# Head strips of queries and keys built by four 32-row products at a time, and q, k, v projections as three single-pass products

## The chip, the cores and the metric

## The reference

For each of 8 batch entries of 512 tokens x 256 features:

```
c   = x[b] @ cond_weight[id_b].T + cond_bias[id_b]        # weights chosen by entry
q, k, v = c @ W_Q, c @ W_K, c @ W_V                       # 16 heads of 16
att = softmax(q k^T / 4 + causal mask) v ;  x1 = x[b] + att @ W_o
h   = LoRA-FFN(x1): relu(x1 wi^T + low rank) wo^T + low rank, rank-16 parts chosen by entry
out = x1 + mixture of 8 experts of h, top 2 by a softmax gate (three layers, gelu)
```

## The kernel before, in words

Stage A is one pass per batch entry, called a round. `Round(b)` computes attention of entry b and, beside it, the FFN and the gate of entry p = b-1; there are nine rounds (round 0 has no FFN, round 8 no attention). Stage B sorts the tokens by expert, stage C runs the experts on tiles of 128 rows. The change touches stage A alone.

A round has an **opening** and then 35 attention **steps**. The opening is a hand-written list (`opening()`): `q0, k0, x1t0, x1t1, q1, k1, v0, qs0, ks0, low_i, qs1, ks1, v1, qs2, ks2, qs3, ks3`, and then four times `hid(j), qs(4+j), ks(4+j)`. Every engine walks this list in order. Item by item:

- `q`, `k` (m = 0, 1): transposed projections, 128 features x 512 tokens, two fp32 products each of `wq_raw` or `wk_sb` with `cond`, the conditioned input of this entry. ScalarE writes the high part into `parts`, VectorE then the low part, which frees the bank.
- `x1t`: output projection of the previous entry (fp32, `wo_sb` x `ot_sb`); VectorE adds the residual, ScalarE takes the high part `x_high`, VectorE the low part `x_low`.
- `v` (0, 1): two tiles of 128 tokens, fp32, four products of 256 columns; ScalarE copies them to `v_sb`.
- `qs`, `ks` (0 to 7): a strip holds two heads, 64 rows each, and repeats high and low parts so that a score product of 64 rows adds all cross terms. A strip is made by two F32R products of 512 columns with a 0/1 selection matrix `sel_sb` of 128 rows, in which only 32 rows are not zero, against `parts` (128 rows). ScalarE copies the q strips, VectorE the k strips.
- `low_i` (four F32R products of 512 columns) and `hid` (seven of them): low-rank input and hidden blocks of the FFN. ScalarE copies `low_i` first, VectorE then writes its low half; `hid` 0 waits for that. Each `hid` is taken by ScalarE (relu, high part) and then by VectorE (low part).

Between these, at places 0 and 10 of the list, ScalarE does one `cast`: it rounds a 128x512 piece of expert weights (`w_rest` to `w_high`, L961) that GpSimd has loaded. GpSimd then subtracts, writes both parts to memory and only after that loads the next piece; the cast waits for that load (`s_wpiece`). At the start of rounds 1 to 7 ScalarE also does six LoRA casts (`lora_high`) ahead of everything in the opening, and VectorE four subtractions.

A **step** has for two heads: two bf16 mask products, two score products of 64 rows (one on rows 0 to 63, the next on rows 64 to 127), transposes of earlier probabilities (L802), a piece of filler work (the rest of the FFN, and `next`: `cond` of the next entry), and every other step probabilities times v. VectorE takes row maxima (`nmax`, L1238), ScalarE the exponential (`probs`, L1060). The first score waits until all strips and v have left PSUM.

Banks are dealt out by `psum_plan`: the opening takes banks 0, 1, 2, 3, 7 in turn; a product waits (`vacant`) until its bank's last content is gone. Scores use banks 0 to 2, fillers 3 and 7, transposes 4 and 5, probabilities times v bank 6 (`PV_BANK`).

Of the kernel before, what the change touches and what calls it, by code (L numbers as in the profile page):

```python
# [18 lines left out]
F32 = mybir.dt.float32  # L19
# [8 lines left out]
P = 128  # L28
# [61 lines left out]
PT_SLOTS = 6  # L90

# [24 lines left out]
def opening(attends, feeds):  # L116

    strips = [[(w, g) for w in ("qs", "ks")] for g in range(HC)]
    order = [] if feeds else [("cond", o) for o in range(KD)]  # L120
    order += [("q", 0), ("k", 0), ("x1t", 0), ("x1t", 1), ("q", 1), ("k", 1), ("v", 0)]
    order += strips[0] + [("low_i", 0)] + strips[1] + [("v", 1)] + strips[2] + strips[3]
    for j in range(HID_EARLY):
        order += [("hid", j)] + strips[4 + j]
# [4 lines left out]
def psum_plan(attends, feeds, leads):  # L129
# [3 lines left out]
    rings = {"linear": [0, 1, 2, 3, 7], "score": [0, 1, 2], "filler": [3, 7], "t": [4, 5],  # L133
# [68 lines left out]
def build_kernel(nc, xT, x_cond_w, x_cond_b, itok, wq, wk, wv, wo, wi_t, wo_t, lora_at, lora_wb, lora_ao, lora_bo,  # L202
# [8 lines left out]
    with outer:  # L211
# [17 lines left out]
        with attn:  # L229
# [7 lines left out]
            cond = sb("cond", [P, KD, S], F32, attn)  # L237
# [3 lines left out]
        behind_attn = sb("behind_attn", [P, PT_SLOTS - 4, S], F32)  # L241
# [5 lines left out]
        wq_raw = sb("wq_raw", [P, KD, D], F32, part_a)  # L247
        wk_sb = sb("wk_sb", [P, KD, D], F32, part_a)
        wv_sb = sb("wv_sb", [P, KD, D], F32, part_a)
        wo_sb = sb("wo_sb", [P, KD, D], F32, part_a)  # L250

        sel_sb = sb("sel_sb", [P, 4, 4, P], F32R, part_a)
# [36 lines left out]
        with ExitStack() as shared:  # L289
            sel_f = sb("sel_f", [P, 4, 4, P], F32, shared)  # L290
# [21 lines left out]
        weight_space = sb("weight_space", [P, 2 * W_ALL - (PT_SLOTS - 4) * S], F32)  # L312
# [92 lines left out]
        s_prep = sem("s_prep")  # L405
        s_idb = sem("s_idb")
# [94 lines left out]
        def _(sp):  # L501
# [93 lines left out]
            sp.dma_start(wk_sb[:, :, :], wk).then_inc(s_const, 16)  # L595
            sp.dma_start(wv_sb[:, :, :], wv).then_inc(s_const, 16)
            sp.dma_start(id_f[:, :], ident).then_inc(s_const, 16)
            sp.dma_start(mask_f[:, :], maskd).then_inc(s_const, 16)
            sp.dma_start(sel_f[:, :, :, :], sel).then_inc(s_sel_f, 16)
# [46 lines left out]
        def _(pe):  # L646
# [6 lines left out]
            def product(rd, n, piece=None):  # L653
# [19 lines left out]
                elif what in ("q", "k"):  # L673
# [4 lines left out]
                    w = wq_raw if what == "q" else wk_sb  # L678
                    for k in range(KD):
                        ins = mm(dst()[:, :], w[:, k, m * P:(m + 1) * P], cond[:, k, :],  # L680
                                 start=(k == 0), stop=(k == KD - 1))
                elif what == "v":
                    vacant(pe, n, rd)
                    for u in range(2):
                        t = 2 * m + u
                        for k in range(KD):
                            ins = mm(dst()[:, u * D:(u + 1) * D], cond[:, k, t * P:(t + 1) * P], wv_sb[:, k, :],
                                     start=(k == 0), stop=(k == KD - 1))
                elif what in ("qs", "ks"):
# [76 lines left out]
            def turn(rd):  # L766
                b, p = rd.b, rd.p
                for n in rd.opening:
                    if p is None and n == ("q", 0):
                        pe.wait_ge(s_const, 16 * N_CONST)  # L770
                        pe.wait_ge(s_idb, 1)
                        pe.wait_ge(s_prep, 1)
# [183 lines left out]
        def _(act):  # L956
# [6 lines left out]
            def take(rd, n, piece=None):  # L963
# [3 lines left out]
                if what == "cond" or what == "next" and piece == KD - 1:  # L967
# [3 lines left out]
                    ins = nc.scalar.activation(cond[:, m, :], at(n, rd)[:, :], ACT.Identity, bias=bc_sb[:, m:m + 1])  # L971
# [59 lines left out]
            def turn(rd):  # L1031
# [3 lines left out]
                for n in rd.opening:  # L1035
                    if p is None and n == ("q", 0):
# [601 lines left out]
```

## Time and profile before

| | |
|---|---|
| median of 3 runs (lowest, highest) | 1537.2 us (1536.48, 1538.39) |
| the profiled execution: its time, its span | 1538.85 us, 1537.3 us |
| TensorE busy | 1416.1 us, 92% |
| VectorE, ScalarE, GpSimd busy | 864.5, 764.6, 419.1 us |
| mean granted TensorE clock | 0.945 |

A granted clock of 1.00 is 2.4 GHz and 0.50 is 1.2 GHz. In a timeline each row gives start and duration in us, engine, line of the kernel, instruction, out<-in and count; square brackets hold the idle time before it and what ended it. The duration of a matmul includes its way through the array, so products that follow each other densely overlap: the distance between starts is what one costs.

### The profile page before, as it was taken

What the parts mean: (1) busy time and instruction counts of PE and PEld (TensorE: products, weight loads), DVE (VectorE), ACT (ScalarE), POOL (GpSimd) and SP (SyncE); (2) the same over time, 40 slices, a digit from 0 to 9 for tenths busy, and PEclk for the clock granted to TensorE, in tenths of its full rate; (3) what the DMA queues carried; (4) which work ended last, traced back from release to release, by engine and by line L of the source; (5) the groups of instructions that cost most, each with busy time, mean ns of one, the idle gap of its engine ahead of it and who ended that gap; (6) DMA issues with size and microseconds to landing.
All of it is one profiled execution on the core that took longest, in us unless ns stands there. A gap on an engine that the chain in (4) does not pass through costs nothing.

```text
span 1537.3 us, 31909 instructions
## 1 busy us (share of the span) xinstructions
PE 1416.1 (92%) x10169; PEld 1085.2 (71%) x10170; DVE 864.5 (56%) x1927; ACT 764.6 (50%) x2000; POOL 419.1 (27%) x553
## 2 busy tenths in 40 slices
PE   6989999999999999999999998339999999999997
PEld 3556776776776776776776776237878888888886
DVE  2665665665665665665664663464555555555554
ACT  3675665665665665665664663003333333333332
POOL 2222211211211211221221220033344544444442
PEclk9599999999999999999999999659999999999998
DMA  6121222222222222222222220381624222442221
GB/s 237 62 83 56 77 84 90 77 84 90 77 84 90 77 84 90 76 84 90 77 84 69 77 78 28 158 332 35 230 58 142 43 40 50 138 145 40 40 38 13
DMA packets 50642, 138.62 MB, mean 90 GB/s; under 512 B 10515, under 2 KB 29587, under 8 KB 48755
## 3 DMA queue, kind: packets, MB, share of 16 engines
q0 software_dynamic: 28992, 68.35, 16.2%
q1 hardware_dynamic: 21554, 68.97, 12.1%
q8 instruction: 64, 1.05, 0.3%
q14 instruction: 32, 0.25, 0.1%
HBM read 86.82 MB, written 51.38 MB: 90 GB/s over the span
## 4 chain that ended last, share of the span: by engine, by line
PE 83%; DVE 5%; DMA 4%; ACT 3%; issue 3%; POOL 1%; POOLq 0%; SPq 0%; DVEq 0%; ACTq 0%
PE bank L651 68%; PE bank L802 10%; PE bank L895 4%; ACT probs L1060 2%; DMA xg<-hrows,gid 1%; PE bank L887 1%; DMA wsplit<-w_rest 1%; DMA out<-y_sb,sid 1%; DVE nmax L1238 1%; DMA w_rest<-in_w_all 1%; PE bank L810 0%; DVE probs_t L1252 0%; POOL hit_v L1496 0%; ACT w_high L961 0%; POOL w_rest L1476 0%
## 5 line engine op out<-in xcount | busy, mean ns | idle before, releaser
L1060 ACT ACTIVATE probs<-bank,nmax 128x512 f32<-128x512 f32 (+3 forms) x512 | 266.0, 525 | 171.0 <-DVE nmax L1238 169.5
L1238 DVE TENSOR_REDUCE nmax<-bank 128x1 f32<-128x512 f32 (+3 forms) x512 | 227.3, 486 | 209.3 <-PE bank L651 209.0
L1094 ACT ACTIVATE g<-z 128x512 f32<-128x512 f32 x142 | 89.8, 632 | 279.5 <-DVE z L1426 279.5
L1476 POOL TENSOR_TENSOR w_rest<-w_rest,w_high 128x512 f32<-128x512 f32 x64 | 81.4, 1271 | 467.7 <-ACT w_high L961 467.7
L802 PE MATMUL bank<-id_f,probs 128*128 128x128 f32 x1280 | 202.9, 290 | 0.2
L651 PE MATMUL bank<-wst,g1t_high 128*128 x568 | 185.3, 407 | 0.9 <-DVE g1t_low L1414 0.9
L802 PEld LDWEIGHTS bank<-id_f,probs 128*128 128x128 f32 x1280 | 138.4, 143 | 44.0 <-issue 27.0
L1518 POOL DMA_INDIRECT out<-y_sb,sid x71 | 114.3, 1609 | 150.1 <-DVE y_sb L1447 69.1
L1252 DVE COPY probs_t<-bank 128x128 f32<-128x128 f32 (+3 forms) x320 | 140.3, 454 | 9.1 <-PE bank L802 9.1
L1426 DVE TENSOR_TENSOR z<-bank,b_sb 128x512 f32<-128x512 f32 x142 | 98.2, 691 | 72.5 <-PE bank L651 61.1
L651 PEld LDWEIGHTS bank<-wst,g1t_high 128*128 128x128 f32 x568 | 102.2, 190 | 20.8 <-issue 1.1
L651 PE MATMUL bank<-wst,g1t_low 128*128 x284 | 113.0, 398 | 0.0
L651 PE MATMUL bank<-wst,g2t_high 128*128 x568 | 108.4, 290 | 1.5 <-DVE g2t_low L1414 1.5
L651 PE MATMUL bank<-k_sb,q_sb 64*128 64x512 f32 (+3 forms) x512 | 108.8, 422 | 0.0
L651 PE MATMUL bank<-mask_b,id_b 128*128 128x128 bf16 x512 | 83.0, 229 | 21.2 <-ACT probs L1060 10.1
L651 PE MATMUL bank<-probs_t,v_sb 128*32 128x128 f32 x2560 | 102.3, 289 | 0.0
L1060 ACT ACTIVATION_READ_ACCUMULATOR probs<-bank,nmax 128x1 f32 x512 | 101.4, 198 | 0.0
L651 PE MATMUL bank<-wst,xgt_high 128*128 x284 | 96.0, 420 | 1.3 <-DVE xgt_low L1414 1.1
L1508 POOL DMA_INDIRECT xg<-hrows,gid x71 | 76.0, 1071 | 63.9 <-POOL gid L1505 57.7
L1068 ACT COPY probs_t<-bank 128x384 f32<-128x384 f32 (+3 forms) x192 | 88.3, 460 | 6.8 <-PE bank L802 6.8
L651 PEld LDWEIGHTS bank<-mask_b,id_b 128*128 128x128 bf16 x512 | 35.3, 98 | 79.7 <-issue 50.4
L1473 POOL DMA_DIRECT2D w_rest<-in_w_all x64 | 34.8, 544 | 206.4 <-DMA wsplit<-w_rest 206.4
(193 smaller groups left out, 2921.2 us busy)
## 6 DMA issues: line engine op xcount, KB each, us to landing
wst<-wsplit SPq DMA_DIRECT2D x8, 4096.0 KB, 12.5
w_rest<-in_w_all POOLq DMA_DIRECT2D x64, 256.0 KB, 3.0
wsplit<-w_high POOLq DMA_DIRECT2D x64, 256.0 KB, 2.3
wsplit<-w_rest POOLq DMA_DIRECT2D x64, 256.0 KB, 2.6
hrows<-h_sb SPq DMA_DIRECT2D x8, 528.0 KB, 3.0
x_in<-in_xT SPq DMA_DIRECT2D x8, 512.0 KB, 3.5
wb_raw<-in_lora_wb SPq DMA_DIRECT2D x8, 512.0 KB, 3.5
x_res<-in_xT SPq DMA_DIRECT2D x8, 512.0 KB, 3.3
```

The lines of the kernel that those rows point to most:

```text
L651: return nc.tensor.matmul(*a, **k)
L802: ins = nc.tensor.transpose(at(n, rd)[:, kb * P:(kb + 1) * P], probs[:, t % 4, kb * P:(kb + 1) * P], id_f[:, :])
L895: ins = nc.tensor.transpose(bank[bt][:, k * P:(k + 1) * P], g[:, k * P:(k + 1) * P], id_f[:, :])
L1060: taken(nc.scalar.activation(probs[:, s % 4, 0:(i + 1) * P], at(n, rd)[:, 0:(i + 1) * P], ACT.Exp, bias=nmax[:, s % 8:s % 8 + 1], accum_ou ...
L1068: taken(nc.scalar.copy(probs_t[:, t % PT_SLOTS, 0:w], at(n, rd)[:, 0:w]), n, rd)
L1094: nc.scalar.activation(g[:, :], z[:, :], ACT.Gelu).then_inc(s_g, 1)
L1238: V.tensor_reduce(nmax[:, s % 8:s % 8 + 1], at(n, rd)[:, 0:(s // HEADS + 1) * P], AX.X, ALU.max, negate=True).then_inc(s_max, 1)
L1252: taken(V.tensor_copy(probs_t[:, t % PT_SLOTS, 0:w], at(n, rd)[:, 0:w]), n, rd)
L1426: V.tensor_tensor(z[:, :], bank[bl][:, :], bias[:, bass.ds(e, 1), :].rearrange("p o n -> p (o n)"), ALU.add).then_inc(s_z, 1)
L1476: nc.gpsimd.tensor_tensor(w_rest[:, :], w_rest[:, :], w_high[:, :].bitcast(F32), ALU.subtract).then_inc(s_wlow, 1)
L1508: nc.gpsimd.indirect_dma_start(xg[:, buffer, :], None, hrows, bass.IndirectOffsetOnAxis(ap=gid[:, 0:1], axis=0), bounds_check=B * S - 1, o ...
L1518: nc.gpsimd.indirect_dma_start(out_rows, bass.IndirectOffsetOnAxis(ap=sid[:, 0:1], axis=0), y_sb[:, buffer, :], None, bounds_check=B * S - ...
```

## The change

The query and key strips are no longer made one by one. `opening()` puts four of one kind together (`quads`): a strip's selection matrix and its part of `parts` are cut to the 32 rows that count, strip number `pair` of a quad reads rows 32 pair to 32 pair + 31, and the four write four different banks. A quad is eight F32R products of 32 rows x 512 columns, first the four of the high part, then the four of the low part. The order becomes `q0, k0, x1t0, x1t1, q1, k1, v0, qs0-3, low_i, ks0-3, hid0, v1, qs4-7, hid1, ks4-7, hid2, hid3`. The opening's ring has eight banks now. ScalarE copies the strips with even numbers, VectorE those with odd ones. `cast` keeps its places 0 and 10 in the list of single items.

`cond` is kept as `cond_high` (ScalarE) and `cond_low` (VectorE, a new instruction of 128x512 for each of its two blocks per round, which now frees the bank). `wq`, `wk`, `wv` are split into high and low parts once, in round 0 (three ScalarE and three VectorE instructions in place of one VectorE scaling). Each projection product of fp32 becomes three F32R products. The selection matrices shrink from 128x2048 to 128x512. The rest of the diff, not shown, is declarations, the loads' new names and the sizes of shared SBUF spaces.

```diff
@@ -116,12 +117,11 @@
-    strips = [[(w, g) for w in ("qs", "ks")] for g in range(HC)]
+    quads = [[(w, 4 * c + pair) for pair in range(4)] for c in range(KD) for w in ("qs", "ks")]
     order = [] if feeds else [("cond", o) for o in range(KD)]
     order += [("q", 0), ("k", 0), ("x1t", 0), ("x1t", 1), ("q", 1), ("k", 1), ("v", 0)]
-    order += strips[0] + [("low_i", 0)] + strips[1] + [("v", 1)] + strips[2] + strips[3]
-    for j in range(HID_EARLY):
-        order += [("hid", j)] + strips[4 + j]
+    order += quads[0] + [("low_i", 0)] + quads[1] + [("hid", 0), ("v", 1)] + quads[2] + [("hid", 1)] + quads[3]
+    order += [("hid", j) for j in range(2, HID_EARLY)]
     ours = ("cond", "q", "k", "v", "qs", "ks")
...
@@ -130,7 +130,7 @@
-    rings = {"linear": [0, 1, 2, 3, 7], "score": [0, 1, 2], "filler": [3, 7], "t": [4, 5],
+    rings = {"linear": [0, 1, 2, 3, 7, 4, 5, PV_BANK], "score": [0, 1, 2], "filler": [3, 7], "t": [4, 5],
              "pv": [PV_BANK]}
...
@@ -675,24 +687,40 @@
                     vacant(pe, n, rd, [("cond", o) for o in range(KD)] if n == ("q", 0) and p is None else ())
-                    w = wq_raw if what == "q" else wk_sb
+                    if p is None and m == 0:
+                        pe.wait_ge(s_prep, 1 if what == "q" else 2)
+                    w_high, w_low = (wq_high, wq_low) if what == "q" else (wk_high, wk_low)
                     for k in range(KD):
-                        ins = mm(dst()[:, :], w[:, k, m * P:(m + 1) * P], cond[:, k, :],
-                                 start=(k == 0), stop=(k == KD - 1))
+                        for w, x in ((w_high, cond_high), (w_high, cond_low), (w_low, cond_high)):
+                            ins = mm(dst()[:, :], w[:, k, m * P:(m + 1) * P], x[:, k, :],
+                                     start=(k == 0 and w is w_high and x is cond_high), stop=(k == KD - 1 and w is w_low))
                 elif what == "v":
                     vacant(pe, n, rd)
+                    if p is None and m == 0:
+                        pe.wait_ge(s_prep, 3)
                     for u in range(2):
                         for k in range(KD):
-                            ins = mm(dst()[:, u * D:(u + 1) * D], cond[:, k, t * P:(t + 1) * P], wv_sb[:, k, :],
-                                     start=(k == 0), stop=(k == KD - 1))
+                            for x, w in ((cond_high, wv_high), (cond_high, wv_low), (cond_low, wv_high)):
+                                ins = mm(dst()[:, u * D:(u + 1) * D], x[:, k, t * P:(t + 1) * P], w[:, k, :],
+                                         start=(k == 0 and x is cond_high and w is wv_high),
+                                         stop=(k == KD - 1 and x is cond_low))
                 elif what in ("qs", "ks"):
                     c, pair = divmod(m, 4)
+                    if pair:
+                        return
                     slot = 0 if what == "qs" else 2
-                    vacant(pe, n, rd, [(what[0], c)])
+                    quad = [(what, m + pair) for pair in range(4)]
+                    for pair in range(4):
+                        vacant(pe, quad[pair], rd, [(what[0], c)] if pair == 0 else ())
                     for u in range(2):
-                        ins = mm(dst()[:, :], sel_sb[:, slot + u, pair, :], parts[:, c, slot + u, :],
-                                 start=(u == 0), stop=(u == 1))
+                        for pair in range(4):
+                            rows = slice(PART * pair, PART * (pair + 1))
+                            ins = mm(at(quad[pair], rd)[:, :], sel_sb[rows, slot + u, :], parts[rows, c, slot + u, :],
+                                     start=(u == 0), stop=(u == 1))
+                            if u == 1:
+                                done(ins, quad[pair], rd)
+                    return
                 elif what == "low_i":
...
@@ -968,7 +995,9 @@
                     filled(act, n, rd)
-                    ins = nc.scalar.activation(cond[:, m, :], at(n, rd)[:, :], ACT.Identity, bias=bc_sb[:, m:m + 1])
+                    nc.scalar.activation(cond_high[:, m, :], at(n, rd)[:, :], ACT.Identity, bias=bc_sb[:, m:m + 1]
+                                         ).then_inc(s_cond_high, 1)
+                    return
                 elif what in ("q", "k"):
...
@@ -979,9 +1008,9 @@
                         ins = nc.scalar.copy(v_to[:, :, half, :, half, :], v_ps[:, :, half, :, :])
-                elif what == "qs":
+                elif what in ("qs", "ks") and m % 2 == 0:
                     filled(act, n, rd)
-                    ins = nc.scalar.copy(q_sb[:, m, :], at(n, rd)[:, :])
+                    ins = nc.scalar.copy((q_sb if what == "qs" else k_sb)[:, m, :], at(n, rd)[:, :])
                 elif what == "x1t":
...
@@ -1038,9 +1067,13 @@
                         act.wait_ge(s_vzero, 1)
+                        nc.scalar.activation(wq_high[:, :, :], wq_raw[:, :, :], ACT.Identity, scale=DH ** -0.5
+                                             ).then_inc(s_prep_high, 1)
+                        nc.scalar.copy(wk_high[:, :, :], wk_raw[:, :, :]).then_inc(s_prep_high, 1)
+                        nc.scalar.copy(wv_high[:, :, :], wv_raw[:, :, :]).then_inc(s_prep_high, 1)
                     if p is None and n == ("qs", 0):
                         act.wait_ge(s_sel_f, 16)
-                        nc.scalar.copy(sel_sb[:, :, :, :], sel_f[:, :, :, :]).then_inc(s_sel, 1)
+                        nc.scalar.copy(sel_sb[:, :, :], sel_f[:, :, :]).then_inc(s_sel, 1)
                     take(rd, n)
...
@@ -1125,9 +1158,6 @@
             V = nc.vector
-            dve.wait_ge(s_const, 16 * N_CONST)
-            V.tensor_scalar(wq_raw[:, :, :].rearrange("p k n -> p (k n)"), wq_raw[:, :, :].rearrange("p k n -> p (k n)"),
-                            DH ** -0.5, None, ALU.mult).then_inc(s_prep, 1)
             dve.sem_inc(s_hout, 1)
...
@@ -1153,15 +1183,19 @@
                 b, p = rd.b, rd.p
-                if what in ("q", "k"):
+                if what == "cond" or what == "next" and piece == KD - 1:
+                    dve.wait_ge(s_cond_high, (b if what == "cond" else b + 1) * KD + (m + 1))
+                    ins = V.scalar_tensor_tensor(cond_low[:, m, :], at(n, rd)[:, :], bc_sb[:, m:m + 1],
+                                                 cond_high[:, m, :].bitcast(F32), ALU.add, ALU.subtract)
+                elif what in ("q", "k"):
                     slot = 0 if what == "q" else 2
                                                  at(n, rd)[:, :], ALU.mult, ALU.add)
-                elif what == "ks":
+                elif what in ("qs", "ks") and m % 2 == 1:
                     filled(dve, n, rd)
-                    ins = V.tensor_copy(k_sb[:, m, :], at(n, rd)[:, :])
+                    ins = V.tensor_copy((q_sb if what == "qs" else k_sb)[:, m, :], at(n, rd)[:, :])
                 elif what == "low_i":
...
@@ -1218,6 +1252,12 @@
                 for before, n in zip([None] + rd.opening, rd.opening + [None]):
+                    if p is None and n == ("q", 0):
+                        for w, (low, raw, high) in enumerate(((wq_low, wq_raw, wq_high), (wk_low, wk_raw, wk_high),
+                                                              (wv_low, wv_raw, wv_high))):
+                            dve.wait_ge(s_prep_high, w + 1)
+                            V.scalar_tensor_tensor(low[:, :, :], raw[:, :, :], DH ** -0.5 if w == 0 else 1.0,
+                                                   high[:, :, :].bitcast(F32), ALU.mult, ALU.subtract).then_inc(s_prep, 1)
                     if n == ("low_i", 0):
...
@@ -1613,8 +1653,7 @@
-        "sel": _np.stack([_np.stack([_np.kron(_np.eye(4)[:, pair:pair + 1], _np.kron(_np.eye(2),
-                                              _np.kron(rows, _np.eye(DH)))) for pair in range(4)], axis=1)
+        "sel": _np.stack([_np.tile(_np.kron(_np.eye(2), _np.kron(rows, _np.eye(DH))), (4, 1))
                           for rows in ([[1, 0, 1, 0]], [[0, 1, 0, 1]], [[1, 1, 0, 0]], [[0, 0, 1, 1]])],
```

## Rows read from the trace of the kernel before

**Rows 1.** The page: busy time of TensorE, and the clock in 40 slices.

```profile
PE 1416.1 (92%) x10169; PEld 1085.2 (71%) x10170; DVE 864.5 (56%) x1927; ACT 764.6 (50%) x2000; POOL 419.1 (27%) x553
...
PEclk9599999999999999999999999659999999999998
```

**Rows 2.** Windows: stretch; busy us of PE, PEld, DVE, ACT, POOL; clock, DMA share, GB/s.

```profile
39.20:76.80 37.60, 36.28 (x223) 21.37 (x223) 25.08 (x72) 24.79 (x92) 8.68 (x12) 0.50 0.18 63
226.90:233.80 6.90, 6.15 (x27) 2.63 (x20) 3.69 (x12) 4.76 (x9) 0.00 (x0) 0.51 0.30 94
238.00:261.00 23.00, 21.83 (x89) 16.39 (x87) 11.86 (x18) 10.55 (x21) 3.45 (x5) 1.00 0.24 85
```

**Rows 3.** Timeline of TensorE in the opening of round 2 and its first steps.

```profile
228.48 3.75 PE L651 MATMUL bank<-cond,wq_raw 128*128 128x512 f32 x4 [0.75 <-issue]
...
234.61 3.60 PE L651 MATMUL bank<-ot_sb,wo_sb 128*128 128x512 f32 x8
238.05 1.88 PE L651 MATMUL bank<-cond,wq_raw 128*128 128x512 f32 x4
...
245.06 1.09 PE L651 MATMUL bank<-parts,sel_sb 128*128 128x512 f32 x4
245.98 1.89 PE L651 MATMUL bank<-wv_sb,cond 128*128 128x256 f32 x8
...
258.75 1.08 PE L651 MATMUL bank<-parts,sel_sb 128*128 128x512 f32 x4
261.12 0.27 PE L651 MATMUL bank<-mask_b,id_b 128*128 128x128 bf16 x2 [1.29 <-DVE k_sb L1164]
...
262.37 0.38 PE L651 MATMUL bank<-mask_b,id_b 128*128 128x128 bf16 x2
```

**Rows 4.** Timeline of TensorE in steps: score pairs and what stands around them.

```profile
198.84 0.50 PE L651 MATMUL bank<-k_sb,q_sb 64*128 64x512 f32 x2
199.28 0.88 PE L802 MATMUL bank<-id_f,probs 128*128 128x128 f32 x6
199.91 0.36 PE L651 MATMUL bank<-wf_high,hid_high 128*128 128x256 f32 x1
200.11 0.28 PE L651 MATMUL bank<-wf_low,hid_high 128*128 128x256 f32 x1
...
200.71 0.46 PE L651 MATMUL bank<-mask_b,id_b 128*128 128x128 bf16 x2
...
264.14 0.28 PE L651 MATMUL bank<-mask_b,id_b 128*128 128x128 bf16 x2
264.35 0.33 PE L651 MATMUL bank<-k_sb,q_sb 64*128 64x128 f32 x2
264.61 0.33 PE L802 MATMUL bank<-id_f,probs 128*128 128x128 f32 x1
```

**Rows 5.** Timeline of the weight loads of one of these score pairs.

```profile
198.84 0.19 PEld L651 LDWEIGHTS bank<-k_sb,q_sb 64*128 64x128 f32 x2
```

**Rows 6.** Timeline of ScalarE, VectorE and GpSimd in round 2.

```profile
233.78 0.62 ACT L961 CAST w_high<-w_rest 128x512 fp32r<-128x512 f32 x1
...
216.96 1.29 DVE L1238 TENSOR_REDUCE nmax<-bank 128x1 f32<-128x512 f32 x2 [1.65 <-PE bank L651]
...
245.88 0.68 DVE L1168 SCALAR_TENSOR_TENSOR low_i<-bank,low_i 32x512 fp32r<-32x512 f32 x1 [0.86 <-ACT low_i L991]
...
240.39 0.54 POOL L1473 DMA_DIRECT2D w_rest<-in_w_all  x1 [2.77 <-DMA wsplit<-w_rest]
```

**Rows 7.** The page: loads of expert weight pieces, KB each, us to landing.

```profile
w_rest<-in_w_all POOLq DMA_DIRECT2D x64, 256.0 KB, 3.0
```

**Rows 8.** Timeline of round 0, TensorE and ScalarE.

```profile
16.00 1.96 PE L651 MATMUL bank<-cond,wq_raw 128*128 128x512 f32 x4 [1.93 <-ACT mask_b L1039]
...
37.80 0.27 PE L651 MATMUL bank<-mask_b,id_b 128*128 128x128 bf16 x2 [0.98 <-DVE k_sb L1164]
...
25.40 1.91 ACT L1043 CAST sel_sb<-sel_f 128x2048 fp32r<-128x2048 f32 x1
```

More of the change, by code:

```diff
@@ L90 @@
 PT_SLOTS = 6
+BEHIND = PT_SLOTS - 4 + KD
 def place_of(h):
@@ L236, in build_kernel @@
             x_in = sb("x_in", [P, KD, S], F32, attn)
-            cond = sb("cond", [P, KD, S], F32, attn)
+            cond_high = sb("cond_high", [P, KD, S], F32R, attn)
+            cond_low = sb("cond_low", [P, KD, S], F32R, attn)
         with ExitStack() as weights:
@@ L240, in build_kernel @@
         attn_space = sb("attn_space", [P, 2, 2, W_ALL], F32)
-        behind_attn = sb("behind_attn", [P, PT_SLOTS - 4, S], F32)
+        behind_attn = sb("behind_attn", [P, BEHIND, S], F32)
         x_res = sb("x_res", [P, KD, S], F32, part_a)
@@ L246, in build_kernel @@
         bc_sb = sb("bc_sb", [P, KD], F32, part_a)
-        wq_raw = sb("wq_raw", [P, KD, D], F32, part_a)
-        wk_sb = sb("wk_sb", [P, KD, D], F32, part_a)
-        wv_sb = sb("wv_sb", [P, KD, D], F32, part_a)
+        with ExitStack() as shared:
+            wq_raw = sb("wq_raw", [P, KD, D], F32, shared)
+        wq_low = sb("wq_low", [P, KD, D], F32R, part_a)
+        wq_high = sb("wq_high", [P, KD, D], F32R, part_a)
+        with ExitStack() as shared:
+            wk_raw = sb("wk_raw", [P, KD, D], F32, shared)
+        wk_low = sb("wk_low", [P, KD, D], F32R, part_a)
+        wk_high = sb("wk_high", [P, KD, D], F32R, part_a)
+        with ExitStack() as shared:
+            wv_raw = sb("wv_raw", [P, KD, D], F32, shared)
+        wv_low = sb("wv_low", [P, KD, D], F32R, part_a)
+        wv_high = sb("wv_high", [P, KD, D], F32R, part_a)
         wo_sb = sb("wo_sb", [P, KD, D], F32, part_a)
-        sel_sb = sb("sel_sb", [P, 4, 4, P], F32R, part_a)
+        sel_sb = sb("sel_sb", [P, 4, P], F32R, part_a)
         nmax = sb("nmax", [P, 8], F32, part_a)
@@ L289, in build_kernel @@
         with ExitStack() as shared:
-            sel_f = sb("sel_f", [P, 4, 4, P], F32, shared)
+            sel_f = sb("sel_f", [P, 4, P], F32, shared)
         hid_low = sb("hid_low", [P, KF, S], F32R, part_a)
@@ L309, in build_kernel @@
         part_a.close()
-        weight_space = sb("weight_space", [P, 2 * W_ALL - (PT_SLOTS - 4) * S], F32)
+        weight_space = sb("weight_space", [P, 2 * W_ALL - BEHIND * S], F32)
         tri_f = sb("tri_f", [P, P], F32)
@@ L405, in build_kernel @@
         s_prep = sem("s_prep")
+        s_prep_high = sem("s_prep_high")
+        s_cond_high = sem("s_cond_high")
         s_idb = sem("s_idb")
@@ L594, in _ @@
             load_in(0, e0)
-            sp.dma_start(wk_sb[:, :, :], wk).then_inc(s_const, 16)
-            sp.dma_start(wv_sb[:, :, :], wv).then_inc(s_const, 16)
+            sp.dma_start(wk_raw[:, :, :], wk).then_inc(s_const, 16)
+            sp.dma_start(wv_raw[:, :, :], wv).then_inc(s_const, 16)
             sp.dma_start(id_f[:, :], ident).then_inc(s_const, 16)
             sp.dma_start(mask_f[:, :], maskd).then_inc(s_const, 16)
-            sp.dma_start(sel_f[:, :, :, :], sel).then_inc(s_sel_f, 16)
+            sp.dma_start(sel_f[:, :, :], sel).then_inc(s_sel_f, 16)
             sp.dma_start(wo_sb[:, :, :], wo).then_inc(s_mid, 16)
@@ L771, in turn @@
                         pe.wait_ge(s_idb, 1)
-                        pe.wait_ge(s_prep, 1)
                     if p is None and n == ("qs", 0):
```

## Prediction

> **What bounds the kernel now.** I read the page first: TensorE is busy 92% of the span, and its clock reads 9 in all slices but two, so this engine paces the kernel [rows 1]. Then I took windows over stage A. In the opening of round 2 the clock is full and TensorE busy for 21.8 of 23.0 us, ScalarE for 10.6 and VectorE for 11.9 [rows 2]: every microsecond taken from TensorE there counts until one of the other two is late. The windows also show two kinds of half-clock stretches. One of 37.6 us covers the attention of round 0, which has no filler work. One of 6.9 us lies over the start of round 2, behind the sparse end of round 1, and loses 3.4 us; rounds 3 to 7 each have one of the same length [rows 2]. Last I read the timeline of one opening. Between q0 at 228.48 and the second step's masks at 262.37 TensorE stands still once, 1.29 us before the first score, for the last k strip: VectorE copies it behind the low part of `hid` 3 [rows 3]. That point, 33.9 us after q0, is where I compare.
>
> **Prices.** Four full-width single-pass products take 0.92 us, 0.23 each (245.06 to 245.98). Eight records of fp32 products take 3.44 us, 0.43 each (234.61 to 238.05) [rows 3]. Single-pass products of 256 columns take 0.12: five between 200.11 and 200.71 [rows 4].
>
> **Projections.** A q or k item is four records, 1.72 us; it becomes six products, 1.38. Four items save 1.36 us per opening. A v item has as many columns, 1.72 us, and becomes twelve products of 256, 1.44; two items save 0.56. The single-pass price is that of the same form of product with the same weight load, so I give this little doubt.
>
> **Strips.** Before, 16 strips are 32 products of 0.23: 7.36 us. For 32-row products there is no row; the nearest are the score pairs, two 64-row products on the two halves of the array. Such a pair needs 0.44 us at 512 columns (198.84 to 199.28) and 0.26 at 128 (264.35 to 264.61) [rows 4]. The 384 columns between cost 0.18, or 0.24 for 512: the price of one product, not of two, so the pair runs at the same time. Its two weight loads take 0.19 us together, the length of one [rows 5], so loads on different rows go together as well. What the pair costs beyond its columns is 0.20 us, and its neighbours pay too: the two masks in front take 0.21 us where two products of 128 columns need 0.11 (264.14 to 264.35), and the first product after the transposes 0.20 where the next ones need 0.12 [rows 4]. A visit to the narrow form costs 0.20 + 0.10 + 0.08 = 0.38 us. A quad is one visit with two rounds of 512 columns: 0.46 + 0.38, about 0.83 us, if four overlap as two do and the second four weights load under the first four products. Four quads: 3.3 us, 4.1 less per opening. Bounds: 0.60 (half the visit hidden) and, if the weights of the four load one after the other at 0.11 (what a transpose costs with its 128-column load: six between 199.28 and 199.91), 8 x 0.11 + 0.38 = 1.2; without any overlap 8 x 0.23 + 0.1 = 1.9. I take 0.83, the value of the pair.
>
> The Trainium skill, "TensorE: Matmul & The Clock Gate", in its part on packing small matmuls, gives 3.07 times for four 32-row products of 512 columns. By it a quad would take 1.84 / 3.07 = 0.60 us and the total below would be 1497; the case has no four-fold row yet.
>
> **What is late next.** I laid the new list out by hand for round 2, with the rows' durations, VectorE to TensorE 0.24 us (as ahead of 261.12), and ScalarE held by its LoRA casts until its cast at 233.78 as before [rows 6]. (The same table for the old list puts the second step's masks at 262.39; the row says 262.37.) TensorE: q0 228.5, k0 231.2 (both mostly at half clock), x1t 233.7, q1 237.2, k1 238.6, v0 239.9, first q quad 241.4, `low_i` 242.2, first k quad 243.1, done at 243.9. Then comes `hid` 0, and it waits for the low half of `low_i`. Before, three strip pairs and v1 lay between; now only one quad does. The chain: ScalarE has the second cast at place 10, ahead of its `low_i` copy. The piece's load is issued 240.39 and lands after 3.0 us, 243.4 [rows 6, 7], 14.9 us after q0. Cast 0.5 us, `low_i` copy 0.6, VectorE's low half 0.69, semaphore 0.24: `hid` 0 starts at 245.5 instead of 243.9, a new stall of 1.6 us. Then `hid` 0, v1, quad, `hid` 1, quad and `hid` 2, 3 run without gaps to 255.0; all banks they need were copied out over 0.5 us before. The strips' copies lie under `hid` 2 and 3, so the old wait of 1.29 us goes. The second step comes sooner than its bank: VectorE must write the low part of `hid` 3 (to 256.4) before the first row maximum, the exponential ends near 257.1, and the second step's masks wait about 0.9 us, to 257.2. So 262.4 becomes 257.2: 5.1 us in round 2. By terms: 1.36 + 0.56 + 4.1 + 0.4 (1.3 wait to 0.9) less 1.6, and 0.3 for the part saved at half clock.
>
> The same table for the other rounds, each with its own half-clock stretch: 5.1, 5.1, 4.6, 4.9, 4.5 us in rounds 3 to 7. Round 1 has no half-clock stretch, reaches `hid` 0 about 2.4 us earlier after q0 and so waits 4.0 us for the same load: 2.6 us saved. Sum of rounds 1 to 7: 31.8 us.
>
> **Round 0.** Here the list has no FFN work. The preparation grows: three ScalarE casts of 0.5 us behind the mask cast and VectorE's first low part put q0 at 17.3 instead of 16.00. The four items and v0 then end at 24.2. The selection cast, 1.91 us before the first strip, falls to 0.6 [rows 8]. From 25.7 the quads are paced by the copies, four banks each, two copies on VectorE at 0.61, and end in a first score at 32.9 instead of 37.80: 4.9 us. The pauses may let the clock fall before the first score and not after 1.4 us of it, 0.4 less. I take 4.5.
>
> **Hidden at no price.** VectorE's two `cond_low` per round (0.69 each) fall into steps where it idles 1.65 us between maxima [rows 6]; if that cover were gone, 0.7 us each, 10 us in all. Later drains of the `next` banks delay nothing that is due within 2 us. Splitting the weights is counted in round 0. Stages B and C keep their code. A smaller selection load only frees DMA time. More banks in the opening cost nothing: the transposes' banks and bank 6 are idle then.
>
> **Sum.** 31.8 + 4.5 = 36.3 us. The profiled execution took 1538.85 us (span 1537.3 and 1.55 around it), which gives 1502.5; the median of the runs lies 1.65 lower, so 1500.9.
>
> **Rivals.**
> 1. *All removed work shows.* If the load lands earlier, or the copies pass faster, so that `hid` 0 doesn't wait, an opening saves 6.4 + 0.3 us: 7 x 6.7 + 5 = 52, 1485. For it: TensorE had no such wait before. Against: the chain is 2.0 us long behind the load with one quad of 0.83 as cover. A half-clock stretch that disappears from the rounds' starts (3.4 us each) would mostly be eaten by the same wait.
> 2. *The four overlap in part.* Weight loads in series, 1.2 us a quad: rounds 1 to 7 save 25.2, 1507.5. No overlap, 1.9 us: 11.6, 1521. For it: a transpose costs its weight load, not its columns; against: [rows 5].
> 3. *Slower: weights exposed.* If the products go one by one and each load (0.19) stands in front, a quad takes 8 x 0.42 + 0.38 = 3.7 us, 1.9 more than before. Per opening 7.5 lost against 2.3 saved by the rest: 7 x 5.2 - 4.5 = 32 slower, 1569. It turns slower once a quad costs over about 2.5 us. Against: both rows of the score pairs.
> 4. *Slower: the clock.* The new waits (4.0 us in round 1, 1.6 later) stand in a stretch that was dense; what precedes each fall of the clock now is a sparse piece of some us. One stretch as in [rows 2] costs 3.4 us; slower than before needs over 5.2 us per opening, that is two of them in each of seven, about 1545. For it: round 0's attention stayed at half clock for 37.6 us. Against: after 1.29 us of idling at 261.12 the clock stayed at 1.00. One extra stretch in round 1 alone is inside my range.
> 5. *PSUM copies pace the opening.* If every quad had to wait for copies, it would cost two VectorE copies, 1.22 us, instead of 0.83: 1.6 more per opening, 11 in all, 1512. Against: VectorE has 21 passes of 0.61 and 2.3 us of LoRA in the new opening, 15 of 28.7 us, so I expect this in round 0 alone. The Trainium skill, "TensorEngine Tiling (Array Packing)", section "PSUM Bottleneck", warns that the copies can become the bound once TensorE is four times as fast.
>
> **How the numbers follow.** Forecast 0.59, with its own range 1493 to 1509 (quad 0.60 to 1.2, clock edges moved by one stretch or two); all work shows 0.14; partial overlap 0.13; copies 0.03; no change 0.02; clock 0.05; exposed weights 0.04. The range 1484 to 1518 takes in the first two, the copies and most of the partial overlap, and leaves out about 0.15. 0.2% (3 us) is what a measurement can tell. Faster 0.89, same 0.02, slower 0.09.
>
> **What would show it.** A quad: start of its first product to the next item, 0.83 us. A gap before `hid` 0 of 1.6 us (4 in round 1), ended by VectorE's `low_i`. No gap before the first score, 0.9 us before the second step's masks. q0 of round 0 at 17.3, its first score at 32.9. Rounds 2 to 7 some 111 us apart instead of 116. The prediction is wrong if the quad's products don't overlap, if half-clock stretches multiply or vanish, or if attention steps get longer by VectorE's new work.

## The result, and the profile after

The changed kernel takes 1527.4 us at the median (1519.1 to 1533.3, 11 runs), the kernel before 1538.0 in the same series (11 runs). The ratio is 0.9926, with an interval of 0.9903 to 0.995: some 11 us are gained where 36 were forecast. The interval leaves out 1.000, so there is a gain, but the time lies outside the range of the prediction, on its slow side. Below, times are compared by such ratios.

The profiled execution took 1528.85 us with a span of 1527.2, 10.1 us less than before. The page of it, first TensorE's busy time and then the clock in 40 slices, answers to [rows 1]:

```profile
PE 1377.0 (90%) x10297; PEld 1069.8 (70%) x10298; DVE 874.2 (57%) x1945; ACT 764.4 (50%) x2003; POOL 419.2 (27%) x553
...
PEclk8799999999999999999999999559999999999999
```

TensorE is busy 39 us less, but the span shrinks by a quarter of that: TensorE now stands where it did not. The timeline of TensorE in the opening of round 2 shows where, and answers to [rows 3]:

```profile
225.32 0.77 PE L663 MATMUL bank<-cond_high,wq_high 128*128 128x512 f32 x1 [0.76 <-issue]
...
237.04 0.28 PE L663 MATMUL bank<-wv_high,cond_low 128*128 128x256 f32 x1
237.25 0.74 PE L663 MATMUL bank<-parts,sel_sb 32*128 32x512 f32 x8
237.93 0.50 PE L663 MATMUL bank<-x_high,at_cat 128*128 128x512 f32 x1
238.26 0.40 PE L663 MATMUL bank<-x_low,at_cat 128*128 128x512 f32 x1
...
239.06 0.74 PE L663 MATMUL bank<-parts,sel_sb 32*128 32x512 f32 x8
244.79 0.77 PE L663 MATMUL bank<-x_high,wi_high 128*128 128x512 f32 x1 [4.99 <-issue]
...
256.25 0.28 PE L663 MATMUL bank<-mask_b,id_b 128*128 128x128 bf16 x2
...
257.53 0.23 PE L663 MATMUL bank<-mask_b,id_b 128*128 128x128 bf16 x1
258.51 0.23 PE L663 MATMUL bank<-mask_b,id_b 128*128 128x128 bf16 x1 [0.76 <-ACT probs L1093]
258.67 0.33 PE L663 MATMUL bank<-k_sb,q_sb 64*128 64x128 f32 x2
```

Ahead of `hid` 0 (244.79) TensorE stands for 4.99 us; the forecast had 1.6. Of the second step's two mask products the first starts at 257.53, and the second waits for its bank to 258.51, 33.19 us after q0, where 28.7 was forecast. The score behind them is the place where like can be compared with like. It starts 33.35 us after q0, and in the kernel before, in the row below, 34.20:

```profile
262.68 0.33 PE L651 MATMUL bank<-k_sb,q_sb 64*128 64x128 f32 x2
```

So the opening of round 2 gains 0.85 us and not 5.1. Over rounds 1 to 7 the wait ahead of `hid` 0 is 4.60, 4.99, 4.59, 3.30, 1.20, 4.46 and 3.86 us. "Issue" says only that the profile names no releaser; ScalarE and VectorE show it. Their timelines, in round 2:

```profile
242.86 0.62 ACT L988 CAST w_high<-w_rest 128x512 fp32r<-128x512 f32 x1 [3.77 <-DMA w_rest<-in_w_all]
243.38 0.59 ACT L1020 ACTIVATE low_i<-bank 128x512 fp32r<-128x512 f32 x1
...
244.00 0.68 DVE L1202 SCALAR_TENSOR_TENSOR low_i<-bank,low_i 32x512 fp32r<-32x512 f32 x1 [4.67 <-ACT low_i L1020]
```

The chain is the one of the prediction: load, cast, `low_i` copy, low half, `hid` 0. But the load is late. GpSimd's timeline answers to [rows 6], and SyncE's follows it:

```profile
233.93 0.54 POOL L1521 DMA_DIRECT2D wsplit<-w_rest  x1
239.78 0.54 POOL L1513 DMA_DIRECT2D w_rest<-in_w_all  x1 [5.32 <-DMA wsplit<-w_rest]
```

```profile
233.95 0.34 SPq L541 DMA_DIRECT2D x_res<-in_xT  x1
```

GpSimd issues the next piece's load only when its two writes have landed. It waits 5.32 us for them where it waited 2.77 [rows 6], and so the load leaves 14.46 us after q0 instead of 11.91. The second write goes out at 233.93. The 512 KB load of the residual, `x_res`, is issued at 233.95, behind the last reader of `x_res`. In the kernel before it was issued 10.56 us after q0, behind the writes; now it is at 8.63 us, on top of them. The table of DMA issues for 225 to 245 gives the landing times: the write took 5.1 us, and 2.6 at the same place before.

```profile
x_res<-in_xT SPq DMA_DIRECT2D x1, 512.0 KB, 4.4
...
wsplit<-w_rest POOLq DMA_DIRECT2D x1, 256.0 KB, 5.1
w_rest<-in_w_all POOLq DMA_DIRECT2D x1, 256.0 KB, 3.0
```

The second loss is the clock. Windows of round 2, columns as in [rows 2]: while TensorE stands the granted clock falls to 0.50 and stays there for 6.8 us, 3.9 of them with work.

```profile
235.40:242.00 6.60, 4.39 (x35) 2.90 (x33) 3.04 (x5) 2.31 (x5) 0.54 (x1) 0.99 0.50 153
241.90:248.70 6.80, 3.91 (x11) 3.29 (x12) 1.97 (x3) 2.62 (x5) 2.35 (x3) 0.50 0.23 86
248.70:256.30 7.60, 7.60 (x48) 5.39 (x47) 4.56 (x7) 4.04 (x9) 0.54 (x1) 1.00 0.11 35
```

A stretch of half clock stands at this place in rounds 1, 2, 3, 4, 6 and 7, of 3.4 us in rounds 1 and 4 and of 6.8 us in the others. The kernel before has none there. Round 5 is the exception: its q0 fell 0.9 us into the half-clock stretch at the round's start, so 6.0 us of it came behind q0 (2.9 in round 2), TensorE reached x1 later, and `x_res` was issued 10.04 us after q0, behind the writes. GpSimd's timeline of it, then TensorE's:

```profile
582.36 0.54 POOL L1513 DMA_DIRECT2D w_rest<-in_w_all  x1 [2.79 <-DMA wsplit<-w_rest]
```

```profile
587.50 0.47 PE L663 MATMUL bank<-x_high,wi_high 128*128 128x512 f32 x1 [1.20 <-issue]
```

There the load leaves at 11.92, `hid` 0 starts at 17.06 (forecast: 17.0), no stretch follows, the waiting mask product comes at 28.98 after q0, and the score behind it 4.5 us sooner after q0 than before. The forecast had 4.6. One round in seven went as predicted.

### The profile page after: what moved, and what is told of

Same layout as the page of the kernel before. It is cut to its first block, busy times and chain, and to the rows that moved or that the text cites. A ratio compares the mean times of both kernels' runs of the same rounds, so it can differ in the third digit from the quotient of the medians.

```text
span 1527.2 us, 32247 instructions
## 1 busy us (share of the span) xinstructions
PE 1377.0 (90%) x10297; PEld 1069.8 (70%) x10298; DVE 874.2 (57%) x1945; ACT 764.4 (50%) x2003; POOL 419.2 (27%) x553
## 4 chain that ended last, share of the span: by engine, by line
PE 80%; DMA 5%; DVE 5%; issue 5%; ACT 4%; POOL 1%; POOLq 0%; SPq 0%; DVEq 0%; ACTq 0%
PE bank L663 65%; PE bank L829 9%; PE bank L922 4%; ACT probs L1093 2%; DMA wsplit<-w_rest 1%; DMA w_rest<-in_w_all 1%; DMA out<-y_sb,sid 1%; PE bank L914 1%; DMA xg<-hrows,gid 1%; DVE nmax L1278 1%; PE bank L837 0%; POOL hit_v L1536 0%; DVE probs_t L1292 0%; POOL w_rest L1516 0%; ACT w_high L988 0%
```

## The experiments

No experiment leaves out part of the computation. The theory, A: TensorE waits for the cast behind a late load, the load is late by the `x_res` collision, and the clock falls because TensorE stands. The rivals: the cast's place is not the point, the collision is not, or the 32-row products themselves bring the clock down.

**1. The cast late.** The opening's second `cast` goes from place 10 of the list to place 17, right behind v1. ScalarE has then copied `low_i` and `hid` 0 before it waits for the load.

```diff
-W_OPENING = (0, 10)
+W_OPENING = (0, 17)
```

> The changed kernel with one edit: ScalarE's second cast of an expert weight piece moves from place 10 of the opening's list (behind the first quad) to place 17 (behind v1). Base: ratio 0.9926 to the kernel before, 1527 us; TensorE waits 27.1 us in all ahead of hid 0 in rounds 1 to 7 (1.2 to 5.0 each) and six half-clock stretches that the kernel before does not have begin at those waits (17.1 us lost). Theory A (ScalarE stands at the cast for the piece's load, low_i's copy is queued behind it, and the clock falls because TensorE stands still): the wait ahead of hid 0 falls to about 1.1 us per round, the second half-clock stretch of rounds 1 to 7 is gone, 19 + 17 = 36 us less, about 1491, ratio 0.970. Theory B (the low_i chain is too long for one quad of cover whatever the cast does): the waits stay, ratio 0.99. Theory C (the clock falls because the 32-row quads count for little, not because of the waits): waits go, the half-clock stretches stay, about 1508, ratio 0.981.

Measured: 0.9702 (0.9676 to 0.9727). The wait ahead of `hid` 0 is 0.78 us in every round, and no half-clock stretch follows it; TensorE's timeline and a window, round 2:

```profile
241.03 0.47 PE L663 MATMUL bank<-x_high,wi_high 128*128 128x512 f32 x1 [0.78 <-issue]
```

```profile
241.00:248.00 7.00, 6.97 (x45) 5.16 (x46) 3.79 (x6) 4.21 (x10) 1.69 (x2) 1.00 0.00 0
```

Against the changed kernel that is 2.2%, some 34 us, three times what the change had brought. In the profiled executions, which differ by 32.5 us of span, the waits ahead of `hid` 0 are 21.5 us shorter in sum, and the half clock behind them, worth 12.3 us, is gone. Two smaller parts are not the wait's: the half-clock stretches at the starts of rounds 2 to 7 last 27.3 us in sum instead of 37.5, worth up to 5 us, and the half clock of round 0's attention lasts longer, so that round 1 starts 5.8 us later.

**2. The residual's load late.** It waits for the copies of x1 in the attention steps too, which puts it some 48 us after q0, far behind GpSimd's writes; the cast stays at place 10.

```diff
+                    wait_for(rd, free, x1s, v_x1)
                     if rd.b is not None:
                         wait_for(rd, free, x1ts, v_x1t)
                         load_res(rd.b)
-                    wait_for(rd, free, x1s, v_x1)
```

> The changed kernel with one edit: SyncE issues the 512 KB load of x_res for the next round behind its wait for the x1 copies (in the attention steps) and not right after x1t has been taken, where it now falls 0.02 us behind GpSimd's second write of a weight piece. The cast keeps place 10. Theory A (that load delays the writes, GpSimd waits 4 to 5 us for them where it waited 2.8 before, and the piece's load and the cast come later): GpSimd's wait returns to 2.8 us, the load lands 14.9 us after q0, the wait ahead of hid 0 is 4.0 us in round 1 and about 1.6 in rounds 2 to 7, 13.5 us less in all, and the half-clock stretches of rounds 2 to 7 go with it (15 us): about 1499, ratio 0.975. Rival (the writes are slow for another reason): no change, 0.9926.

Measured: 0.9839 (0.9813 to 0.9865), 0.9% or some 13 us better than the changed kernel, but less than expected. That the collision held the writes up is shown: GpSimd's wait falls to 2.76 to 2.78 us in six of seven rounds, and in these the cast starts 14.8 to 15.0 us after q0, as forecast (13.8 in round 1). In round 2 the wait is 3.74 us with no `x_res` near; what held that write up stays open. Round 3, where q0 is at 337.99: GpSimd, ScalarE, TensorE, and windows.

```profile
349.89 0.54 POOL L1513 DMA_DIRECT2D w_rest<-in_w_all  x1 [2.76 <-DMA wsplit<-w_rest]
```

```profile
352.95 0.62 ACT L988 CAST w_high<-w_rest 128x512 fp32r<-128x512 f32 x1 [0.99 <-DMA w_rest<-in_w_all]
```

```profile
354.88 0.47 PE L663 MATMUL bank<-x_high,wi_high 128*128 128x512 f32 x1 [2.22 <-issue]
```

```profile
354.80:358.80 4.00, 3.92 (x13) 3.35 (x14) 1.64 (x3) 0.82 (x2) 1.21 (x3) 0.57 0.37 135
358.80:364.80 6.00, 6.00 (x40) 4.21 (x39) 3.52 (x6) 3.49 (x8) 0.54 (x1) 1.00 0.13 44
```

What the expectation missed: the wait of 2.1 to 3.1 us that is left still brings half clock behind it, in every one of the seven rounds, each stretch 3.4 us long. With the load landing as forecast (rounds 3 to 7) TensorE waits 2.07 to 2.44 us and not 1.6, and half clock follows. What a wait of 1.6 us would do in an opening no run shows.

**3. The wait filled.** 18 extra products of 512 columns stand ahead of `hid` 0, into its bank; their result is overwritten. TensorE then doesn't stand, but nothing is done sooner.

```diff
+FILL = 18
...
+                    if m == 0 and b is not None:
+                        vacant(pe, n, rd)
+                        for _ in range(FILL):
+                            mm(dst()[:, :], wi_high[:, 0, 0:P], x_high[:, 0, :], start=True, stop=True)
```

> The changed kernel with 18 extra F32R products of 512 columns (4.1 us, result overwritten) on TensorE right ahead of hid 0 in rounds 1 to 7, into hid 0's own bank. Nothing else moves. Theory A (the clock falls because TensorE stands still for 4 to 5 us): the half-clock stretches behind this place are gone, 17 us, and the products cost only in round 5, where the wait is 1.2 us (3 us more): about 1513, ratio 0.984. Theory C (the clock falls for the quads' sake): the stretches stay, about 1530, ratio 0.995.

Measured: 0.9876 (0.9853 to 0.99). The window over the place where the clock was at 0.50, and the products (the 19th is the first of `hid` 0):

```profile
242.00:248.00 6.00, 6.00 (x38) 4.86 (x37) 2.67 (x4) 3.15 (x7) 2.40 (x3) 1.00 0.24 87
```

```profile
240.10 4.61 PE L664 MATMUL bank<-x_high,wi_high 128*128 128x512 f32 x19
```

The clock stays at 1.00 at this place in all rounds, with the same quads before it. So the standing brings it down, not the narrow products. The whole program gains less than the openings show, because in this execution the half clock of round 0's attention lasts 41.0 us instead of 20.5, which is 10 us lost.

**4. The cast late, and v1 ahead of `hid` 0**, to cover the last 0.78 us.

```diff
-... + quads[1] + [("hid", 0), ("v", 1)] + quads[2] ...
+... + quads[1] + [("v", 1), ("hid", 0)] + quads[2] ...
```

> The edit of e1 (cast at place 17) and v1 put ahead of hid 0 in the opening's list. Theory A: v1's twelve products (1.44 us) cover what is left of the wait for low_i's low half, about 7 us less than e1 over seven rounds: 1484, ratio 0.965. Theory B: no gain over e1.

Measured: 0.9691 (0.9669 to 0.9714). The wait is gone; against experiment 1 the intervals overlap, so a gain is not shown.

**5. The strips alone.** The quads with the cast late, and the projections left in fp32 as before; the edit, not shown, is the strips' part of the change and the cast's place.

> The strips' part of the change alone, with the cast at place 17: quads, their order in the list, eight banks, small selection matrices; the q, k, v projections stay fp32 as before. Theory A (quads measured at 0.68 us in the changed kernel's trace): strips 7.36 to 2.7 us per opening, 1.29 to 0.75 ahead of the attention, about 0.8 given back ahead of hid 0: 4.3 us in each of seven rounds and 4 in round 0, 34 us, about 1505, ratio 0.978. The difference to e1 (0.9702) is then what the projections give: 1.9 us in seven rounds less the later start of round 0. Rival (the projections' products carry the gain): ratio above 0.985.

Measured: 0.979 (0.9762 to 0.9818). The strips with the cast late bring 2.1%. The difference to experiment 1, 0.9%, is the share of the projections; the intervals do not overlap, but the two were measured in different series. The quad stands in the same place in both and costs the same. In this kernel's round 2:

```profile
230.61 1.89 PE L650 MATMUL bank<-wv_sb,cond 128*128 128x256 f32 x8
232.43 0.73 PE L650 MATMUL bank<-parts,sel_sb 32*128 32x512 f32 x8
233.10 0.50 PE L650 MATMUL bank<-x_high,at_cat 128*128 128x512 f32 x1
```

**6. The quad strip by strip.** Experiment 1, with high and low product of a strip behind each other instead of four high ones and then four low ones. If four products on different rows must stand side by side to overlap, this undoes it.

```diff
-                    for u in range(2):
-                        for pair in range(4):
+                    for pair in range(4):
+                        for u in range(2):
```

> e1 with the quad's eight products in another order: both products of strip 0, then both of strip 1, and so on (same instructions, same rows and banks). Theory A (products on different rows run together, two on the same rows one after the other, and TensorE takes them in order): the second product of one strip runs beside the first of the next, five lengths of 0.23 us in place of two, a quad takes about 1.35 us instead of 0.68; 0.7 x 4 x 8 = 21 us more than e1, about 1515, ratio 0.984. Rival (each row group has its own queue, order is indifferent): as e1, 0.970.

Measured: 0.9713 (0.9693 to 0.9733), the same as experiment 1, and the quad takes 0.68 us:

```profile
234.49 0.75 PE L663 MATMUL bank<-parts,sel_sb 32*128 32x512 f32 x8
235.17 0.50 PE L663 MATMUL bank<-x_high,at_cat 128*128 128x512 f32 x1
```

My expectation was wrong and the rival's right: the order inside the group doesn't matter here.

**7. The split of the weights early.** Experiment 4, with ScalarE and VectorE splitting `wq` and `wk` before the first `cond` is ready, and `wv` behind it. The edit, not shown, moves only these instructions and two small casts.

> e4 (cast at place 17, v1 ahead of hid 0) with round 0's preparation moved: ScalarE splits wq and wk and writes the bf16 identity and mask before it takes the first conditioned block, wv right after them, and VectorE's low parts of wq and wk go ahead of cond_low. TensorE waits 3.23 us for wq_low in e4 (q0 at 17.46). Theory: q0 starts about 16.4, 1 us earlier, and the half-clock stretch of 18 to 23 (1.7 us) may go: 1 to 3 us less than e4, ratio 0.967 to 0.969. Rival: the start is set by the cond products and their copies, q0 not earlier than 17.0, no change.

Measured: 0.9671 (0.9651 to 0.969). q0 of round 0 starts at 15.47 at full clock, not at 17.40 at half clock (17.46 in experiment 4). It has now only `cond` to wait for:

```profile
15.47 0.48 PE L663 MATMUL bank<-cond_high,wq_high 128*128 128x512 f32 x1 [1.76 <-DVE cond_low L1189]
```

Round 1 then starts 1.7 us sooner than in experiment 4, within what was expected, but the intervals of the two ratios overlap, so a gain over experiment 4 is not shown.

**8. A control.** The kernel before, with its cast moved to place 17 of its own list, which is `hid` 0; the cast runs behind that copy (the expectation says just ahead of it).

> The kernel before the change, with only the place of the opening's second cast moved: from place 10 of its list to place 17, the place just ahead of its own first hidden block. A control for the experiment that moved the cast in the changed kernel and took it from 0.993 to 0.970. Theory A (the cast's place matters only because the change made TensorE arrive at hidden block 0 early and wait there; before the change three pairs of strips and v1 lay between, and no wait was there): 1.000, between 0.997 and 1.003, and no wait ahead of hidden block 0 as before. Rival (a late cast helps any such opening, by freeing ScalarE for its copies or by another course of the clock): 0.990 or less, the start of the second step then earlier than 30.2 to 33.1 us after the round's start.

Measured: 0.9999 (0.9985 to 1.0013). The move is worth nothing without the quads: three strip pairs and v1 covered the chain there. What experiment 1 gained is thus the price of a wait that the change itself had opened.

**9. Experiment 7, and the residual's load late** as in experiment 2.

> The best version so far (cast late, v1 ahead of hidden block 0, weights of round 0 split earlier; 0.967), and in it the 512 KB residual load issued late as well, behind the same wait as in the earlier experiment. Theory A (the collision of this load with GpSimd's writes costs only through the cast that TensorE waited for; with the cast late nobody waits): 0.967, between 0.964 and 0.970, though GpSimd's wait for its writes falls from about 5 to about 3 us. Rival (the collision also delays later pieces, or holds GpSimd back in the steps): 0.964 or less.

Measured: 0.9629 (0.9612 to 0.9646), which lies below the range of theory A and on the rival's side of the expectation. It is the lowest ratio of this study, 3% below that of the changed kernel. GpSimd's load is issued 11.9 us after q0 again, where experiment 7 had it at 13.4:

```profile
227.90 0.54 POOL L1516 DMA_DIRECT2D w_rest<-in_w_all  x1 [2.76 <-DMA wsplit<-w_rest]
```

The profiled executions of experiments 7 and 9 differ by 0.6 us of span and start rounds 1 to 7 within 0.5 us of each other. So the traces show nothing of what the rival names, a delay of later pieces that costs time, and where the difference of 0.4% between their ratios comes from stays open; the two were measured in different series.

## Why the prediction was wrong, by its own steps

**The failed step** is that of "What is late next", with rival 4 behind it. It took the load as issued 11.9 us after q0, as in the kernel before, and so landing 14.9 after it. The duration was right (3.0 to 3.2 us). The issue was not: in rounds 1 to 7 the load leaves 12.8, 14.5, 14.1, 13.1, 11.9, 14.0 and 13.6 us after q0. I had laid out TensorE, VectorE and ScalarE for the new list, but not SyncE, whose `x_res` load moves forward with x1. The load moves by 1.93 us in round 2: 0.66 for q0 and k0, which are shorter, and some 1.2 because more of the half-clock stretch now lies ahead of q0. The 0.66 alone would have put it at 9.90, and in the kernel before round 7 has it at 9.88 with a wait of GpSimd of 2.85 us, so that much would have passed; the margin was what I should have looked for. The trace of the kernel before had it in round 1, which has no such stretch: q0 is at 115.28, `x_res` is issued 7.96 us after it, and GpSimd already waits 3.86 us there. SyncE, then GpSimd, of the kernel before:

```profile
123.24 0.34 SPq L529 DMA_DIRECT2D x_res<-in_xT  x1
```

```profile
127.11 0.54 POOL L1473 DMA_DIRECT2D w_rest<-in_w_all  x1 [3.86 <-DMA wsplit<-w_rest]
```

The prediction took round 2's load for all rounds. With the load put back to its forecast time (experiment 2) the kernel gains some 13 us, half of what was missing; the other half is the clock, below, and a wait that was longer than 1.6 us even then.

What it cost, in the profiled executions: `hid` 0 was to start 17.0 us after q0 in every round; it starts at 17.77, 19.47, 19.10, 17.99, 17.06, 19.02 and 18.65, 10.1 us late in sum. The waits themselves are longer than forecast by 13.4 us; part of that is only earlier arrival.

**The clock**, rival 4, was no term of the sum: what follows a new wait was put at nothing, and the rival had been given 0.05 with "two of them in each of seven" as its condition for a slower kernel. One in six rounds came. Behind the six waits TensorE works at half clock from `hid` 0 to the rise for 3.4, 3.9, 4.4, 2.9, 4.6 and 5.5 us, which loses half of it, 12.3 us. My argument against it was the 1.29 us of idling ahead of the first score; experiment 2 shows how little that argument covered: 2.07 us were enough, and the 4.0 us that I had forecast for round 1 lay far above that. (The rival's 1545 is a slip besides: two stretches of 3.4 us in seven rounds are 47.6 us, 1548 in all.) The text had named one such stretch, in round 1, as within its range, and not asked why only there.

**The sum.** Late `hid` 0, 10.1; half clock behind it, 12.3; more of the rounds' first half-clock stretches lying ahead of q0, 1.6; round 0, 0.5; stages B and C, 2.3. Together 26.8 us; 1502.5 forecast for the profiled execution and 1528.85 measured differ by 26.3. The last 2.3 us lie in stage C, whose code did not change: from its first product with `wst` to the end the changed kernel takes 500.8 us and the kernel before 498.4. Over the eleven profiled executions of this study, all with the same code there, that part takes 498.1 to 502.2 us, so this is probably a difference between executions.

**The terms that held.** The projections cost 0.23 and 0.12 us a product (in round 2 six of k1 in 1.40 us, from 234.35 to 235.75, and twelve of v0 in 1.41), and are worth 0.9% (experiment 5); 1.92 us by seven rounds is 13.4 us, 0.9%. The quad was priced at 0.83 with what it does to its neighbours. It takes 0.68 from its start to the next item, 0.09 in front (237.04 to 237.25 where 0.12 is a product) and 0.10 behind (237.93 to 238.26 where 0.23 is one): 0.87. The sign named in the prediction, "start of its first product to the next item, 0.83", mixed the two. The quad's 0.68 is 2.7 times as fast as eight products one by one (1.84), and its 0.87 with the neighbours 2.1 times. By the 3.07 times of the Trainium skill, "TensorE: Matmul & The Clock Gate", part on packing small matmuls, the estimate for a quad was 0.60; the trace has 0.68, and the measurement decides. Round 0, where two quads follow each other without a gap, is in line with a price made of a visit and the columns:

```profile
28.64 1.20 PE L663 MATMUL bank<-parts,sel_sb 32*128 32x512 f32 x16 [1.25 <-ACT sel_sb L1076]
```

One quad's row lasts 0.74 us and two last 1.20, so the second adds 0.46, the price of two products for eight. With the wait out of the way (experiment 1) the changes are worth 3.0%; the forecast was 2.4% with 14 us of waits in it.

**The wait before the second step's masks**, forecast 0.9, is 0.75 to 0.76 in all rounds. No round waits ahead of the first score.

**Round 0.** q0 at 17.40 (17.3 forecast), the masks of the first score at 35.14, not at 32.9 (37.80 before): in the pause of 2.79 us ahead of q0 the clock fell, at 16.6, and it rose at 23.4, in a stretch I had taken as full. The half clock of round 0's attention lasts 20.5 us, not 37.5, and another stretch of 6.8 us stands at 84.9. Round 1 starts 4.0 us sooner; I had 4.5. That this is close is in part luck: only 2.7 us were gained by the first score, and the long half-clock stretch behind it differs from execution to execution. In the control (experiment 8), whose round 0 has the work of the kernel before, it lasts 23.9 us and round 1 starts 3.4 us sooner as well.

**The other rivals.** Weights are not exposed: the eight loads of a quad take 0.30 us together. This is the timeline of weight loads, and answers to [rows 5]:

```profile
237.25 0.30 PEld L663 LDWEIGHTS bank<-parts,sel_sb 32*128 32x128 f32 x8
```

Copies pace the openings nowhere but in round 0.

## What to carry to other kernels

When one engine's work is shortened, lay out the new times of every queue, also of those that only issue transfers: a load that moves forward by 2 us can land on a write that somebody waits for. Put an instruction that waits for a transfer behind the copies that the bounding engine needs next; here one number in a list was worth three times the change. A short new wait on TensorE is to be priced with the clock that follows it, in each round and not in one.

## What the runs showed of the hardware that I had not expected

- In a dense stretch, waits of 2.07 to 3.10 us (seven in experiment 2) were each followed by half clock for 3.4 us; waits of 0.78 us (seven in experiment 1), 1.20 us (round 5 of the changed kernel) and 1.28 to 1.32 us (seven in the kernel before) by none. Between them lie only the pauses ahead of round 0's q0, where less stands before them: 1.76 us (experiments 7 and 9) and 1.93 us (the kernel before and the control) left the clock at 1.00, and 2.51 to 3.23 us (six executions) were followed by half clock.
- A wait inside a half-clock stretch costs less than it seems: of the 6.8 us in round 2, 2.9 passed standing.
- Two DMA requests at once: the 256 KB write took 5.1 us instead of 2.6, and the 512 KB load 4.4 instead of 3.1.
- The long half-clock stretch of round 0's attention lasted 37.5 us in the kernel before and 23.9 us in the control, with the same work in round 0.
- Eight products on four row groups take 0.68 us, whether products on the same rows stand next to each other or not.
